# Last expert layer: expert-per-partition logits, an accumulating comparison for each count and one bf16 pass

## The reference, cut to what matters

```python
def _L3_ffn_ref(x, Wg, W1, W2, W3):           # x flattened: n = 4096 tokens, C = 128
    e = Wg.shape[0]                            # 8 experts
    capacity = max(1, int(1.0 * n / e))        # 512 tokens of each expert
    scores = (x_flat @ Wg.T).T                 # (8, 4096)
    top_vals, token_idx = jax.lax.top_k(scores, capacity)
    token_w = jax.nn.softmax(top_vals, axis=-1)
    xg = x_flat[token_idx]
    y = (the expert's gated MLP of xg) * token_w[..., None]
    out = zeros_like(x_flat).at[token_idx.reshape(-1)].add(y.reshape(-1, c))
```

## Time and profile before

| | |
|---|---|
| median of 3 runs | 4113.77 us (4111.6 to 4127.46) |
| span of the profiled execution | 4112.9 us (the profile gives its time by this span alone) |
| PE busy | 3752.4 us, 91% |
| DVE busy | 3216.6 us, 78% |
| ACT busy | 2258.9 us, 55% |
| POOL (GpSimd) busy | 1293.1 us, 31% |
| mean granted TensorE clock | 0.942 of full speed |

### The profile page before, as it was taken

How to read it: one execution, slowest core, us unless ns; L and a number is a source line. 1 busy time by engine, 2 the same in 40 slices (tenths; PEclk the granted TensorE clock), 3 DMA queues, 4 the chain that set the end, 5 groups by cost and what they waited for, 6 DMA issues and landing times.

```text
span 4112.9 us, 77952 instructions
## 1 busy us (share of the span) xinstructions
PE 3752.4 (91%) x25021; PEld 2518.5 (61%) x25021; DVE 3216.6 (78%) x11881; ACT 2258.9 (55%) x6989; POOL 1293.1 (31%) x1092
## 2 busy tenths in 40 slices
PE   7999999999999998999989987988987999899845
PEld 5777777777777776666653433335555666555533
DVE  7888888888888886667768996776885778788661
ACT  5777777778777774226764433433333222477401
POOL 1333333333333331014536875530100000222006
PEclk9999999999999998988999998999997999799758
DMA  2000000000000001211000000000000000000013
GB/s 122 2 2 2 2 2 2 2 2 2 2 2 2 2 2 47 90 58 63 2 2 0 0 10 1 0 0 1 1 1 32 1 1 1 32 2 2 22 53 50
DMA packets 30835, 63.57 MB, mean 15 GB/s; under 512 B 3424, under 2 KB 19808, under 8 KB 29152
## 3 DMA queue, kind: packets, MB, share of 16 engines
q1 hardware_dynamic: 24288, 52.29, 3.6%
q0 software_dynamic: 6144, 6.30, 0.9%
HBM read 49.93 MB, written 8.65 MB: 14 GB/s over the span
## 4 chain that ended last, share of the span: by engine, by line
PE 70%; DVE 16%; issue 7%; ACT 5%; POOL 2%; DMA 1%; DVEq 0%; POOLq 0%; ACTq 0%; SPq 0%
PE ps L473 9%; PE ps L512 9%; PE ps L170 8%; PE ps L454 6%; PE ps L497 5%; PE ps L1584 3%; PE ps L1555 3%; PE ps L1553 3%; PE ps L2158 2%; PE ps L2145 2%; DVE gbbc L2197 2%; PE ps L930 2%; DVE gbbc L2186 2%; DVE gbbc L2192 2%; PE ps L908 2%
## 5 line engine op out<-in xcount | busy, mean ns | idle before, releaser
L598 DVE CUSTOM_DVE_ANT_0 T<-ps,C 128x128 f32<-128x128 f32 x2048 | 451.5, 286 | 1.9
L745 POOL TENSOR_TENSOR W<-W,T 128x512 f32<-128x512 f32 x256 | 261.1, 1041 | 525.1 <-DVE T L634 525.1
L692 ACT ACTIVATE W<-T 128x128 f32<-128x128 f32 x1024 | 395.9, 390 | 46.4 <-DVE T L619 46.4
L745 POOL TENSOR_TENSOR T<-T 128x512 f32<-128x512 f32 x256 | 261.1, 1041 | 483.3 <-DVE T L634 483.3
L473 PE MATMUL ps<-T 64*128 64x128 f32 (+1 forms) x4096 | 404.9, 337 | 4.3 <-DVE T L598 4.2
L473 PEld LDWEIGHTS ps<-T 64*128 64x128 f32 x4096 | 344.1, 187 | 85.8 <-issue 64.5
L692 ACT ACTIVATE T<-T 128x128 f32<-128x128 f32 x1024 | 396.4, 392 | 0.3 <-DVE T L619 0.2
L512 PE MATMUL ps<-W,gbbc 128*64 128x256 f32 x3072 | 388.1, 388 | 3.1 <-ACT T L709 3.1
L609 DVE COPY_PREDICATED W<-gbbc,ps 128x512 f32<-128x512 int32 x512 | 342.9, 722 | 38.6 <-PE ps L170 38.6
L170 PE MATMUL ps<-C,T 128*128 128x128 f32 (+1 forms) x1617 | 263.1, 300 | 50.0 <-DVE T L301 19.0
L1157 POOL TENSOR_TENSOR QK<-T,QK 128x512 fp32r<-128x512 f32 x128 | 162.1, 1276 | 379.1 <-ACT T L1117 262.1
(11 more groups left out here) (408 smaller groups left out, 8755.0 us busy)
## 6 DMA issues: line engine op xcount, KB each, us to landing
T<-crow_dram SPq DMA_DIRECT2D x128, 128.0 KB, 3.0
W<-in_l1f_dram SPq DMA_DIRECT2D x1, 6152.0 KB, 18.3
W<-in_l0a_dram SPq DMA_DIRECT2D x1, 5172.5 KB, 25.6
W<-in_l2f_dram SPq DMA_DIRECT2D x1, 3160.0 KB, 10.4
W<-in_l3f_dram SPq DMA_DIRECT2D x1, 3076.0 KB, 9.9
W<-in_sm_dram SPq DMA_DIRECT2D x1, 2729.0 KB, 9.7
W<-in_l0f_dram SPq DMA_DIRECT2D x1, 2256.0 KB, 30.2
X<-in_x_dram SPq DMA_DIRECT2D x1, 2048.0 KB, 8.2
```

Source lines behind the costliest of these rows:

```text
L598: done(e.tensor_tensor_reduce(sm[:, at:at + 128], src, m, 1.0, -3.0e38, ALU.add, ALU.max, mx[:, col:col + 1]), s["masked"], x == (3 if ban ...
L692: done(e.activation(a.Pr[i % 4][:, at:at + w_], a.Sm[i % 2][:, at:at + w_], ACT.Exp, bias=a.ngs[i % 4][:, c:c + 1], scale=a.scale, accum_o ...
L745: e.tensor_tensor(pr, pr, a.rins[i % 4][:, c:c + 4].unsqueeze(2).broadcast_to([P, 4, 128]), ALU.mult).then_inc(s["norm"].sem, 1)
```

## The change

Only the last expert layer is touched.

- **Logits.** GpSimd builds `spread`, 128x144 zeros in which the gate matrix stands at every 16th column from column 15 on. For batch b of 256 tokens a window of it that begins at column 15 - b is the weight of one fp32 matmul over 256 columns of HT; all 16 matmuls accumulate into the same 128x256 of bank 4. Partition 16 e + b then holds the 256 logits of expert e in batch b: an expert has 16 partitions, and a threshold is one number for each partition.
- **Count.** One `tensor_scalar` compares 128x256 with a candidate that is a [128, 1] operand and accumulates along the row (`accum_out`). The sum of a partition is at most 256, so the upper half of its fp32 word is exact as bf16; PE multiplies it by `same`, a bf16 block matrix of ones (16x16 blocks), one column wide.
- **Next states.** The state of the search is a pair (threshold so far, candidate). While PE counts, DVE writes the pairs for both outcomes; after the answer one comparison with the target makes a mask of two columns and one predicated copy takes the right pair.
- **Maximum.** It is no longer ahead of the counts: a row maximum is taken while the first count is on PE, PE turns it, DVE reduces it during the second count, and GpSimd does the subtraction.
- **Back to the old layout.** PE transposes the 128x256 logits twice ahead of the first count, ACT copies them into S in the old order, and at the end PE turns the threshold and the two comparisons read it from PSUM.
- **Work between counts.** PE's transposes and gate rows come in halves, two after each count from count 3 to 26. The tokens are written to `hrow_dram` ahead of the gate.

```diff
@@ -1194,7 +1200,13 @@
     def batch(b):
         if b == 0:
             e.wait_ge(*f.ends[1])
+            if f.l == 3:
+                e.wait_ge(*f.s["spread_out"](1))
         e.wait_ge(*k.s_h(16 * f.no + b + 1))
+        if f.l == 3:
+            done(e.matmul(k.bank[4][:, 0:256], f.spread[:, 15 - b:143 - b], k.HT[:, 256 * b:256 * b + 256], start=(b == 0),
+                          stop=(b == NB - 1)), f.s["logits"], b == NB - 1)
+            return
         for i in (2 * b, 2 * b + 1):
             done(e.matmul(k.bank[4][:, n * i:n * i + n], k.HT[:, 128 * i:128 * i + 128], wg, start=True, stop=True),
                  f.s["logits"], i == NT - 1)
@@ -1705,7 +1717,10 @@
     f.w = views(k.W1, L3F)
     f.hrow, f.flat = k.hrow, k.out.rearrange("b t d -> (b t) d")
     f.S, f.Y, f.A, f.E0 = r.many(4, 256)
-    f.sg, f.kk, f.t, f.cd, f.pr, f.thr, f.mx, f.need, f.c8, f.top = r.many(10, 8)
+    f.mx, f.need, f.c8 = r.many(3, 8)
+    f.rows, f.crow = r.get(256), r.get(2)
+    f.sg, f.kk, f.pr, f.thr, f.mrow, f.zero = r.many(6, 1)
+    f.state, f.ways, f.mask = r.get(2), r.many(2, 4), r.get(2)
     f.two, f.run, f.dst, f.pre = r.many(4, 512)
     f.back, f.rest, f.slot = r.many(3, 256)
     f.parts = [r.get(128).bitcast(BF16) for _ in range(3)]
...
+    f.spread, f.block, f.same = free.get(144), free.get(128), free.get(64).bitcast(BF16)
...
-    f.s |= sems(k, "p", asked=COUNTS + 4, answered=COUNTS + 4, shifted=1, numbers=1, numbered=1, turned=16, taken=16, split=1,
+    f.s |= again(k, "soft", by_pool=("gather", 2), by_dve=("sel", 4), by_pe=("mT", 3), stored=("mb", 1))
+    f.s |= sems(k, "p", asked=COUNTS + 2, answered=COUNTS + 2, shifted=1, numbers=1, numbered=1, turned=16, taken=16, split=1,
                 spread=1, one=NT, found=NT, place=1, ys=8)
+    nth = lambda n, i: Sig(f.s[n].sem, f.s[n].base + i)
+    f.s |= {"spread_out": nth("by_pool", 0), "built": nth("by_pool", 1)}
+    f.s |= {"placed": nth("by_dve", 0), "peaked": nth("by_dve", 1), "top": nth("by_dve", 2), "edged": nth("by_dve", 3)}
+    f.s |= {"mirrored": nth("by_pe", 0), "peaks": nth("by_pe", 1), "edge": nth("by_pe", 2)}
...
 def pick_rows(k, f, e):
 
+    e.wait_ge(*f.s["taken"](8))
+    e.dma_start(f.hrow.rearrange("(i p) d -> p i d", p=128)[:, :, 0:128],
+                f.hx.rearrange("p (i d) -> p i d", d=128)).then_inc(f.d_row, 16)
     e.wait_ge(*k.s_rows(4 * f.gate.no + 4))
     for j in range(2):
         e.dma_start(f.hrow.rearrange("(b t p) d -> p b t d", t=2, p=128)[:, :, j, 128:256],
                     k.gbbc[:, :].rearrange("p (b d) -> p b d", d=128)).then_inc(f.d_row, 16)
-    e.wait_ge(*f.s["taken"](8))
-    e.dma_start(f.hrow.rearrange("(i p) d -> p i d", p=128)[:, :, 0:128],
-                f.hx.rearrange("p (i d) -> p i d", d=128)).then_inc(f.d_row, 16)
-
-
-def pick_back(k, f, e, g):
+
+
+def pick_back(k, f, e, g, js):
 
     past(e, f.s["taken"], g - 3)
-    for j in range(4):
+    for j in js:
         i = 4 * g + j
         done(transpose(k, e, k.bank[g % 4][:, 128 * j:128 * j + 128], k.HT[:, 128 * i:128 * i + 128]), f.s["turned"], j == 3)
 
@@ -1760,22 +1781,34 @@
     s, w, banks = f.s, f.w, (k.bank[5], k.bank[6])
     for sem, v in f.ends:
         e.wait_ge(sem, v)
-    e.wait_ge(*s["asked"](1))
-    transpose(k, e, banks[0][0:8, 0:128], f.mx).then_inc(s["answered"].sem, 1)
-    e.wait_ge(*s["asked"](2))
-    e.matmul(banks[1][:, 0:8], k.C["ones"][0:8, :], f.top[0:8, :], start=True, stop=True).then_inc(s["answered"].sem, 1)
-    e.matmul(k.bank[7][:, 0:128], k.C["ones"], k.C["tri"], start=True, stop=True)
-    e.matmul(k.bank[7][:, 128:256], k.C["tri"], k.C["ones"], start=True, stop=True).then_inc(s["numbers"].sem, 1)
+    e.wait_ge(*s["placed"](1))
+    for j in range(2):
+        done(transpose(k, e, k.bank[4][:, 256 + 128 * j:384 + 128 * j], f.rows[:, 128 * j:128 * j + 128]), s["mirrored"], j == 1)
+    e.wait_ge(*s["built"](1))
     for n in range(COUNTS):
-        e.wait_ge(*s["asked"](n + 3))
-        e.matmul(banks[n % 2][:, 0:8], k.C["ones"], f.c8, start=True, stop=True).then_inc(s["answered"].sem, 1)
-        if 1 <= n <= 8:
-            pick_back(k, f, e, n - 1)
-        elif 9 <= n <= 12:
-            if n == 9:
+        e.wait_ge(*s["asked"](n + 1))
+        e.matmul(banks[n % 2][:, 0:1], f.same, f.crow[:, n % 2:n % 2 + 1].bitcast(BF16)[:, 1:2], start=True,
+                 stop=True).then_inc(s["answered"].sem, 1)
+        if n == 0:
+            e.wait_ge(*s["peaked"](1))
+            transpose(k, e, k.bank[3][:, 0:128], f.mrow.broadcast_to([P, 128])).then_inc(s["peaks"].sem, 1)
+        elif n == 1:
+            e.matmul(k.bank[7][:, 0:128], k.C["ones"], k.C["tri"], start=True, stop=True)
+        elif n == 2:
+            e.matmul(k.bank[7][:, 128:256], k.C["tri"], k.C["ones"], start=True, stop=True).then_inc(s["numbers"].sem, 1)
+        elif n <= 18:
+            if n == 3:
+                e.wait_ge(*s["top"](1))
+            pick_back(k, f, e, (n - 3) // 2, (0, 1) if n % 2 else (2, 3))
+        elif n <= 26:
+            if n == 19:
                 e.wait_ge(*s["taken"](8))
-            gate_rows_pe(k, f.gate, e, (n - 9,), (k.bank[4], k.bank[3]))
-    e.wait_ge(*s["asked"](COUNTS + 3))
+                e.wait_ge(*s["stored"](1))
+            gate_rows_pe(k, f.gate, e, ((n - 19) // 2,), (k.bank[4], k.bank[3]), (0, 1) if n % 2 else (2, 3))
+    e.wait_ge(*s["edged"](1))
+    e.wait_ge(*k.s_rows(4 * f.gate.no + 4))
+    transpose(k, e, k.bank[3][:, 0:128], f.thr.broadcast_to([P, 128])).then_inc(s["edge"].sem, 1)
+    e.wait_ge(*s["asked"](COUNTS + 1))
     e.matmul(banks[0][:, :], k.C["tri"], f.two, start=True, stop=True)
     e.matmul(banks[1][:, :], k.C["ones"], f.two, start=True, stop=True).then_inc(s["answered"].sem, 1)
     e.wait_ge(*s["numbered"](1))
...
+    e.wait_ge(*s["mirrored"](1))
+    for j in range(2):
+        done(e.activation(f.S.rearrange("p (b j e) -> p j e b", j=2, e=8)[:, j],
+                          k.bank[4][:, 256 + 128 * j:384 + 128 * j].rearrange("p (e b) -> p e b", b=16), ACT.Copy, bias=0.0,
+                          scale=1.0), s["stored"], j == 1)
...
 def pick_dve(k, f, q):
     c_, s, banks = k.cd, f.s, (k.bank[5], k.bank[6])
     S, Y, A, E0 = f.S, f.Y, f.A, f.E0
-    sg, kk, t, cd, pr, thr, mx, need, c8 = f.sg, f.kk, f.t, f.cd, f.pr, f.thr, f.mx, f.need, f.c8
+    sg, kk, pr, need, c8 = f.sg, f.kk, f.pr, f.need, f.c8
     e_t = lambda ap: ap.rearrange("p (t e) -> p e t", e=8)
     over = lambda ap: ap.unsqueeze(1).broadcast_to([P, NT, 8])
+    of_expert = lambda bank: bank[:, 0:128].rearrange("p (e b) -> p e b", b=16)
     for sem, v in f.ends:
         q.wait_ge(sem, v)
+    c_.then(q.memset(f.zero, 0.0))
+    c_.then(q.memset(f.state, 0.0))
     q.wait_ge(*s["logits"](1))
-    c_.then(q.tensor_copy(S, k.bank[4][:, 0:256]))
-    c_.hold(q)
-    q.tensor_reduce(mx, e_t(S), AX, ALU.max).then_inc(s["asked"].sem, 1)
-    q.wait_ge(*s["answered"](1))
-    c_.then(q.tensor_reduce(thr[0:8, 0:1], banks[0][0:8, 0:128], AX, ALU.max))
-    c_.hold(q)
-    q.tensor_scalar(f.top[0:8, 0:8], k.C["ident"][0:8, 0:8], thr[0:8, 0:1], None, ALU.mult).then_inc(s["asked"].sem, 1)
-    q.wait_ge(*s["answered"](2))
-    c_.then(q.tensor_copy(mx, banks[1][:, 0:8]))
-    c_.hold(q)
-    q.tensor_tensor(v3(E0, 8), v3(S, 8), over(mx), ALU.subtract).then_inc(s["shifted"].sem, 1)
+    q.tensor_copy(f.rows, k.bank[4][:, 0:256]).then_inc(s["placed"].sem, 1)
+    q.wait_ge(*s["placed"](1))
     n = [0]
 
-    def count(src3, against):
+    def count(values, against):
         c_.hold(q)
-        c_.then(q.tensor_tensor(v3(A, 8), src3, over(against), ALU.is_ge))
-        c_.hold(q)
-        q.tensor_reduce(c8, e_t(A), AX, ALU.add).then_inc(s["asked"].sem, 1)
+        q.tensor_scalar(A, values, against, None, ALU.is_ge, ALU.add,
+                        accum_out=f.crow[:, n[0] % 2:n[0] % 2 + 1]).then_inc(s["asked"].sem, 1)
         n[0] += 1
-        q.wait_ge(*s["answered"](n[0] + 2))
-        return banks[(n[0] - 1) % 2][:, 0:8]
-
-    c_.then(q.memset(t, 0.0))
-    c = count(v3(S, 8), t)
+
+    def counted():
+        q.wait_ge(*s["answered"](n[0]))
+        return banks[(n[0] - 1) % 2][:, 0:1]
+
+    count(f.rows, f.zero)
+    q.tensor_reduce(f.mrow, f.rows, AX, ALU.max).then_inc(s["peaked"].sem, 1)
+    c = counted()
     c_.then(q.tensor_scalar(pr, c, 511.5, None, ALU.is_ge))
     c_.hold(q)
     c_.then(q.tensor_scalar(sg, pr, 2.0, -1.0, ALU.mult, ALU.add))
     c_.then(q.tensor_scalar(kk, pr, 512.0 - 3585.0, 3585.0, ALU.mult, ALU.add))
     c_.hold(q)
-    c_.then(q.tensor_tensor(v3(Y, 8), v3(S, 8), over(sg), ALU.mult))
-    ti, ci, pi = t.bitcast(I32), cd.bitcast(I32), pr.bitcast(I32)
+    c_.then(q.tensor_scalar(Y, f.rows, sg, None, ALU.mult))
+    now = f.state
+    c_.then(q.tensor_scalar(now[:, 1:2].bitcast(I32), now[:, 0:1].bitcast(I32), 1 << 30, None, ALU.bitwise_or))
     for bit in range(30, -1, -1):
+        count(Y, now[:, 1:2])
+        way = f.ways[bit % 2]
```

(41 more changed lines are left out.)

12 lines of the change are left out of this document (7 added, 5 removed).

## The result

| | before | after |
|---|---|---|
| median of 4 runs each on one chip | 4112.69 us (4111.47 to 4127.46) | 4064.65 us (4063.93 to 4065.05) |
| span of the profiled execution | 4112.9 us | 4063.3 us |
| DVE busy | 3216.6 us | 3194.1 us |
| PE busy | 3752.4 us | 3736.1 us |
| mean granted clock | 0.942 | 0.949 |

The ratio of the times is 0.9874, 95% interval 0.9854 to 0.9894: faster, by more than the 0.5% that the chances were given for. The forecast was 4073.0, and its range ended at 4065: the measured time lies 8.35 us under the forecast and 0.35 us under the range. The direction and the mechanisms of the savings were right, several sizes were not, and one slowing of DVE was missing. Which ones, the stages tell.

A forecast was written before the change was run, and what follows sets the result against it. The search was taken as bound by a closed chain of DVE and PE, repeated for 31 bits. 33.5 - 0.8 + 3.1 + 1.1 - 0.5 = 36.4, plus 4.8 for the logits, 41.2 saved: 4073 us, range 4065 to 4088.

The forecast's parts named there:

- the bit: Search, each of 31 bits: comparison 0.50, PE's answer 0.31, two small operations 0.40, plus 0.05; 1.26 us, saving 33.5 us.
- the rise of the clock in the logits: Last layer's logits: PE's clock rises 6 us after wide matmuls begin, at about 3866, as in the experts; 4.8 us saved.
- the added 0.05: Search, each bit: allowance because the two next-state operations fit into PE's 0.31 us answer only if they overlap.
- The side work: PE's halved transposes and gate matmuls between counts: transposes hide under 1.26, gate matmuls just not; 8 x 0.1 = 0.8 us lost.
- Ahead of the counts: Between logits' copy and first bit: 3.1 us saved to the first comparison, 1.1 from there to the first bit's.
- At the end: After the search, PE turns the threshold: 0.46 us, taken as 0.5 us lost.
- The write of the normalized tokens: `pick_rows` waits for tokens first; their write takes 12 us to land, well before GpSimd wants them; nothing lost.
- The low clock: Rival: in the logits the clock stays at 0.50, giving -1.5 us in place of +4.8; 4078.9 us, chance 0.33.
- Two elements a cycle: Rival: the accumulating comparison takes 0.37 us, saving 4.0 us more over 31 bits; 4068.6 us, chance 0.12.
- Nothing overlaps: Rival: comparison, read-out and next states all run ahead of PE's answer, 1.90 us a bit; 4098.7 us, chance 0.08.
- PE never waited for `spread_out`: Slower rival: PE waits for GpSimd's weights ahead of the first logits; 4123.6 us if 51 us late, chance 0.02.
- a little sooner: Range's lower end: 4066.4 us from the bit's lower end, with a clock rise in the logits slightly earlier, reaching 4065.

The follow-up runs named there:

- the half count: Against the changed kernel, each count's comparison reads 128 of its 256 columns, leaving out half of the scores; 4066.66 us in one run.

## Why the prediction was right, and where it was not

In short: two terms of the sum were mis-sized, the bit (1.26 where 1.16 were measured, 3.1 us over 31 bits) and the rise of the clock in the logits (forecast 6 us after the first wide matmul, measured after 1.4, 2.3 us). Smaller errors lie beside them. That the time fell 0.35 us under the range is itself a matter of chance: 1.53 us of the difference lie ahead of the layernorm, where executions of one kernel scatter by more than 20, and the same kernel's second median, 4085.61, lies inside the range. The stages below don't depend on that.

**The bit: right in its parts, 0.10 too long.** Predicted were 0.50 to the count, 0.31 for PE's answer, 0.40 for two small operations and 0.05 for overlap that might be incomplete, 1.26. Measured are 0.48, 0.29 (0.06 to PE's start, 0.19, 0.04), 0.39, and nothing: 1.16. The largest piece is the added 0.05. It had no row under it, and the trace shows the next states finished 0.09 before PE. 31 x 0.10 = 3.1 us.

**The side work: 0.8 predicted, 0.13 measured.** Of the eight counts with gate matmuls one is longer, 1.29 in place of 1.16. The step that failed was adding half of 2.05 to the whole answer for each count: a count's four records of L271 do take 1.20 as a group at the low clock, but they start 0.05 to 0.07 after the start of the answer, overlap it, and are off PE in time for the next. Only behind the first group, whose records start 0.24 after the start of the answer (3893.22 against 3892.98), is the next answer late. And the low clock holds for half of the counts only: the window from 3896 to 3898 has a mean of 0.60, those from 3898 to 3904 have 1.00, and a group takes 0.69 there.

**What the prediction did not have: GpSimd's exponentials beside the bits**, 0.47 us, in one bit. It called that work harmless since its result is needed 40 us later. That is right for the result and wrong for the operations of DVE beside it: the predicted sum put the slowing of L1940 at nothing. 3.1 + 0.7 - 0.5 is 3.3 of the 3.4 by which the bits, with their side work, were undersold (36.07 against 32.7).

**The logits: the mechanism right, its moment wrong, 2.3 us.** Predicted was a rise 6 us after wide matmuls began, a figure taken from the experts. PE's timeline in after, from the first 256-column matmul on:

```profile
3858.64 1.06 PE L1207 MATMUL ps<-HT,W 128*128 128x256 f32 x2
3859.49 0.63 PE L176 MATMUL ps<-C,T 128*128 128x128 f32 x2
3859.92 0.68 PE L1207 MATMUL ps<-HT,W 128*128 128x256 f32 x2
3860.43 0.38 PE L176 MATMUL ps<-C,T 128*128 128x128 f32 x2
3860.65 0.60 PE L1207 MATMUL ps<-HT,W 128*128 128x256 f32 x2
```

The second pair already takes 0.68 and not 1.06. A mean clock of 0.90 from 3859.66 to 3861.66 puts the rise at 3860.06, 1.4 us after the first wide matmul. Read the same way it comes after 0.9 us in the second trace of after (stage of 12.96), and after 2.3 in the experiment with comparison and sum apart (13.63); the other four traces with wide logits have 0.9 to 1.6. A batch takes 1.28 at the low clock (3858.64 to 3859.92) and 0.65 at the high one, so each microsecond of high clock wins about half a microsecond: a rise 4.6 us sooner than forecast is worth the 2.3 us, and the 0.5 sooner and 0.9 later of the other two traces fit their stages (0.26 shorter, 0.41 longer). So the one event of the earlier trace rows, with other work in front of it, was no measure of the delay, and the trace of before held a second one, 4.1 us in the search, that the prediction did not use. A batch at the high clock has the period that was predicted: 0.65 (3860.43 to 3861.08) against 0.66. The section "Part 1: The HAM clock gate (the "warmup" mystery)" of "TensorE: Matmul & The Clock Gate" in the Trainium skill says that the moment varies between runs of one kernel; the traces agree, with 1.4 and 0.9 us in the two of the changed kernel.

**Ahead of the counts.** The 3.1 from copy to comparison came out at 3.06. From the first comparison to the first bit 1.73 are needed where 2.15 and up to 0.3 were set down: DVE's small operations start 0.07 to 0.19 apart and not 0.20, and the row reduction starts with the read-out. Moving the maximum back in front was not tried alone.

**At the end** the lost time is there, 0.60 from the multiplication to L1948 (0.80 against the 0.20 between L1898 and its next in before). The stretch as a whole is no longer, but it scatters by more than that. The write of the normalized tokens never mattered, as predicted: GpSimd's fetch starts behind the token lists.

```profile
3947.82 0.19 DVE L2021 TENSOR_TENSOR T<-T 128x32 int32<-128x32 f32 x1
...
3948.31 1.19 POOL L2080 DMA_INDIRECT W<-hrow_dram,T  x1 [71.12 <-DVE T L2021]
```

**The rivals.** The low clock is refuted by the windows; it is what the kernel with the old logits does. Two elements a cycle is refuted by the half count. "Nothing overlaps" is refuted by the bit's rows; its own sum was off, since it holds 0.59, the price of two fp32 records, for PE's one, and 0.15 where its text has 0.34 for the next states (0.71 + 0.34 + 0.31 + 0.40 are 1.76 and not 1.90). PE never waited for `spread_out`: GpSimd wrote it at 3819.51, and PE's first matmul with it starts 39 us later.

```profile
3819.51 0.19 POOL L2051 COPY W<-W 128x8 f32<-128x8 f32 x1
```

**The sum.** 3.4 (bits and side work), 2.3 (logits), 0.7 (to the first bit), 0.5 (end) are 6.9 us more than predicted; the 1.5 us ahead of the layernorm are not of the change. Together 8.4, the distance from 41.2 to 49.6. All four errors lie on one side: three of the terms held a margin or an estimate on the slow side (0.05 a bit, 6 us to the rise, up to 0.3 ahead of the first bit), and the sum collected them. The range added the bits' lower end but allowed only 1.4 us for a clock that rises "a little sooner", where 2.3 were measured.

## What to carry to other kernels

In a closed chain of two engines count the gaps and not the busy shares: one accumulating comparison, one bf16 record of PE and operations moved into the wait took a step that runs 31 times from 2.34 to 1.18 us, and nothing else in the change was worth a quarter of it. Give each open term of a sum its likely value and put the doubt into the range, or the margins add up to an error of their own. Where executions of one kernel scatter by 20 us, an effect of 5 us is still readable to 0.1 if the traces are cut at the same instructions and compared stage by stage.

## What the runs showed of the hardware

- A comparison of 256 fp32 elements with accumulation takes 0.48 us, without 0.35, over 128 elements 0.35; the read-out of 0.08 adds nothing behind it.
- One bf16 matmul record with one column takes 0.19, the fp32 pair 0.58, and the pair with eight columns 0.59.
- DVE operations with no semaphore between them start 0.07 to 0.08 apart though each lasts 0.16; one that waits for the result of the one before it starts 0.19 after it.
- While GpSimd works on SBUF, DVE's plain comparison went from 0.35 to 0.91, a predicated copy of two columns from 0.16 to 0.69, a copy from 0.16 to 0.39; the accumulating comparison (0.48) and the row reduction (0.42) did not change.
- The clock rose 0.9 to 2.3 us after the first 256-column matmul in seven executions of wide logits, 5.0 us after it where narrow ones stood between, and 4.1 us after the first 128-column gate matmul in the search of before; with 8-column matmuls, transposes and as busy a PE it stayed at 0.50 for 20 us, twice.
- Two profiled executions of the same program took 4063.3 and 4086.0 us, by what happened ahead of the layernorm, and 207.64 and 207.65 us from there to the end.
